# Another front for a fused conditioning block: the first weight block in halves, the second summed on TensorE, the turn later, and a grouped last bias

## The reference, cut to what matters

```
h = ln(ln(x, pw_g[path], pw_b[path]), cp_g[class], cp_b[class])
t = ln(x, tm_g[class], tm_b[class]);  s = ln(x, ms_g[scale], ms_b[scale])
m, n, r = x + (one row per batch, from three small networks)
cat = [w0*h, w1*t, w2*m, w3*n, w4*r, w5*s]
out = x + ln(silu(cat @ int_W1 + int_b1) @ int_W2 + int_b2, int_g, int_be)
```

## Time and profile before

| what | us |
|---|---|
| runs, median of 3 (lowest, highest) | 931.65 (930.84, 932.00) |
| the profiled execution, its own time | 931.71 |
| its span, first to last instruction | 930.0 |
| PE busy | 920.1 (99%) |
| DVE busy | 825.4 (89%) |
| POOL busy | 478.7 (51%) |
| ACT busy | 327.0 (35%) |

### The profile page before, as it was taken

One profiled execution on the slowest core, in us unless ns is written; L12 is line 12 of the kernel. 1 busy time (PEld: TensorE's weight loads), 2 busy tenths in 40 slices (PEclk: granted clock), 3 DMA queues, 4 the chain that ended last, 5 costly groups with the idle time before them and its releaser, 6 DMA issues.

```text
span 930.0 us, 13476 instructions
## 1 busy us (share of the span) xinstructions
PE 920.1 (99%) x4178; PEld 746.5 (80%) x4178; DVE 825.4 (89%) x1205; ACT 327.0 (35%) x414; POOL 478.7 (51%) x577
## 2 busy tenths in 40 slices
PE   8999999999999999999999999999999999999997
PEld 7777888888888888888888888887888878788885
DVE  7889999798989989899898989989899898989965
ACT  5835234252332514324242333424224242333412
POOL 5456474544736455474644637454473644637240
PEclk9999999999999999999999999999999999999999
DMA  9984666738666574756748566574757648565541
GB/s 334 349 307 153 215 171 244 187 95 262 165 217 176 162 236 132 252 133 239 189 118 262 162 213 160 184 226 121 251 144 243 175 128 254 160 218 155 136 113 45
DMA packets 99619, 178.75 MB, mean 192 GB/s; under 512 B 10129, under 2 KB 49041, under 8 KB 95633
## 3 DMA queue, kind: packets, MB, share of 16 engines
q1 hardware_dynamic: 44512, 95.88, 29.9%
q0 software_dynamic: 22976, 66.07, 27.1%
q10 hardware_dynamic: 32112, 16.58, 6.1%
HBM read 145.75 MB, written 32.75 MB: 192 GB/s over the span
## 4 chain that ended last, share of the span: by engine, by line
DVE 32%; PE 29%; DMA 16%; issue 12%; POOL 4%; ACT 3%; ACTq 2%; DVEq 1%; POOLq 0%; SPq 0%
DMA h_turned<-y_sb 15%; PE hid_ps L1612 7%; PE hid_ps L1614 7%; PE hid_ps L1613 7%; DVE y_sb L1117 4%; DVE yst L1120 4%; DVE r_sb L1216 4%; ACT v_ring L800 3%; DVE xc L1028 3%; DVE hid_lo L1141 3%; DVE v_ring L1080 3%; POOL fve L544 2%; DVE fst L1152 2%; DVE cat_lo L1010 2%; DVE o_sb L1150 2%
## 5 line engine op out<-in xcount | busy, mean ns | idle before, releaser
L1612 PE MATMUL hid_ps<-cat_hi,w_hi 128*128 128x512 f32 x1008 | 395.0, 392 | 0.0
L1614 PE MATMUL hid_ps<-cat_hi,w_lo 128*128 128x512 f32 x1008 | 392.3, 389 | 0.0
L1613 PE MATMUL hid_ps<-cat_lo,w_hi 128*128 128x512 f32 x1008 | 392.3, 389 | 0.0
L1612 PEld LDWEIGHTS hid_ps<-cat_hi,w_hi 128*128 128x128 f32 x1008 | 189.2, 188 | 47.4 <-issue 7.4
L1614 PEld LDWEIGHTS hid_ps<-cat_hi,w_lo 128*128 128x128 f32 x1008 | 189.2, 188 | 39.5
L1613 PEld LDWEIGHTS hid_ps<-cat_lo,w_hi 128*128 128x128 f32 x1008 | 189.3, 188 | 38.6
L617 POOL DMA_INDIRECT pw_rows<-pw,path_now x64 | 73.1, 1142 | 123.4 <-DVE y_sb L1136 106.7
L638 POOL DMA_DIRECT2D r_sb<-x x60 | 57.5, 958 | 135.1 <-DVE r_sb L1216 129.7
L624 POOL DMA_INDIRECT pw_rows<-cp,class_now x64 | 94.7, 1480 | 35.3 <-issue 12.6
L846 ACT ACTIVATE cat_hi<-v_ring 128x1024 fp32r<-128x1024 f32 x30 | 31.9, 1063 | 193.4 <-DMA v_ring<-h_turned 191.8
L838 ACT ACTIVATE cat_hi<-v_ring 128x1024 fp32r<-128x1024 f32 x64 | 66.5, 1060 | 84.6 <-DVE v_ring L1080 37.9
(11 more groups left out here) (197 smaller groups left out, 1378.3 us busy)
## 6 DMA issues: line engine op xcount, KB each, us to landing
x_sb<-xp SPq DMA_DIRECT2D x16, 1024.0 KB
out<-r_sb SPq DMA_DIRECT2D x63, 256.0 KB, 2.0
xc<-xT SPq DMA_DIRECT2D x15, 1024.0 KB
h_turned<-y_sb ACTq DMA_DIRECT2D x60, 256.0 KB
r_sb<-x POOLq DMA_DIRECT2D x60, 256.0 KB, 4.5
v_ring<-h_turned SPq DMA_DIRECT2D x60, 256.0 KB, 2.9
stats_bc<-token_stats SPq DMA_DIRECT2D x15, 512.0 KB, 5.8
ids_sb<-ids SPq DMA_DIRECT2D x16, 256.0 KB
```

The costliest lines, as they stand in the source:

```text
L1612: pe.matmul(acc, w1_hi[:, k, cols], hi, start=start, stop=False)
L1613: pe.matmul(acc, w1_hi[:, k, cols], lo, start=False, stop=False)
L1614: return pe.matmul(acc, w1_lo[:, k, cols], hi, start=False, stop=stop)
```

## The change

It replaces the front. The two loads of weight block 0 become two column halves of all three source blocks (384 KB each); x^T's first half comes as two loads of one feature block. Block 0 is summed, rounded and multiplied in column halves. Block 1 is summed by PE: three f32 matmuls with w2, w3, w4 on a diagonal (`mix_diag`, made by POOL) into `made_ps`; its high and low parts are read from there. Block 2 now stands ahead of `turn_x(0)` on PE, block 3 ahead of `turn_x(1)`; ACT rounds block 2 before it norms x, and block 3 before it copies the turned half. 23 warm matmuls stand first, none later. The last bias becomes four matmuls of 32 rows each, on four row groups, together ahead of `last_second(0)`; POOL prepares it for all 128 rows. In the loop, `out_sum(b-1, 0)` and `out_stats(b-1, 1)` move ahead of `y_mul(b+1, 0)` and `y_mul(b+1, 1)`.

SP, POOL and the constants (the last part is POOL's preparation of the last bias):

```diff
-WARM = (30, 7)
+WARM = 23
+
+HALF = D // 2
...
+        mix_diag = [stats_bc[:, j, 0:P] for j in range(NETS)]
...
-                    sp.dma_start(keep[:, 0, :], blocks[:, 0, :]).then_inc(sum_in[k], 16)
-                    sp.dma_start(keep[:, 1:NETS, :], blocks[:, 1:NETS, :]).then_inc(sum_more_in[k], 16)
+                    for i in range(2):
+                        cols = slice(i * HALF, (i + 1) * HALF)
+                        sp.dma_start(keep[:, 0:NETS, cols], blocks[:, :, cols]).then_inc(part_in[i], 16)
...
+                pool.wait_ge(mix_ready, 1)
+                for j in range(NETS):
+                    pool.tensor_tensor(mix_diag[j], ident, w_mix[:, 2 + j:3 + j].to_broadcast([P, P]), ALU.mult).then_inc(diag_ready, 1)
                 pool.wait_ge(signs_ready, 2)
...
-            pool.memset(class_tab[:, :].bitcast(f32), 0.0).then_inc(b2_cleared, 1)
-            pool.memset(onehot[:, 0:P].bitcast(f32), 1.0).then_inc(b2_cleared, 1)
...
-                pool.tensor_copy(class_tab[at:at + 1, :], b2_bc[at:at + 1, :]).then_inc(b2_rounded, 1)
...
+            pool.memset(onehot[:, 0:P].bitcast(f32), 1.0 / 8).then_inc(b2_cleared, 1)
...
+            pool.tensor_copy(class_tab[:, :], b2_bc).then_inc(b2_rounded, 1)
...
+            pool.tensor_tensor(b2_low, in_cols[0], in_cols[1].bitcast(f32), ALU.subtract).then_inc(b2_rounded, 1)
...
+            pool.tensor_tensor(b2_high, in_cols[1].bitcast(f32), high_rows, ALU.mult).then_inc(b2_rounded, 1)
...
+            pool.tensor_tensor(b2_low, b2_low, low_rows, ALU.mult).then_inc(b2_rounded, 1)
...
+            pool.tensor_tensor(in_cols[1], b2_high, b2_low, ALU.add).then_inc(b2_ready, 1)
```

ACT's order:

```diff
-            sum_first(0)
-            x_high(0, 0)
-            sum_high(0)
-            sum_first(1)
+            part_first(0)
+            x_first_high(0)
+            part_first(1)
+            part_high(0)
+            x_first_high(1)
+            part_high(1)
             x_high(0, 1)
+            sum_high(1)
+            sum_first(2)
             act.wait_ge(table_in, 16)
             act.activation(class_tab[:, :], tab_raw, ACT.Copy).then_inc(tab_rounded, 1)
+            sum_high(2)
             act.wait_ge(tab_rounded, 1)
             act.activation(class_tab[:, :], class_tab[:, :].bitcast(f32), ACT.Copy, scale=tab_sign).then_inc(tab_hi_done, 1)
-            sum_high(1)
-            sum_first(2)
             for t in range(TT - 1):
                 x_norm(t)
-            sum_high(2)
             sum_first(3)
+            sum_high(3)
             xhat_copy(0)
-            sum_high(3)
```

DVE's order in `first_chunk` and in `chunk`:

```diff
-                sum_blocks(0)
-                x_low(0, 0)
-                sum_low(0)
+                part_sum(0)
+                x_first_low(0)
+                part_low(0)
+                part_sum(1)
+                part_low(1)
+                x_first_low(1)
                 gain_signs()
                 for t in range(TT):
                     x_stats(0, t)
-                sum_blocks(1)
                 x_low(0, 1)
                 sum_low(1)
+                sum_blocks(2)
                 x_norm_last()
-                sum_blocks(2)
+                sum_low(2)
                 tab_low()
                 onehot_first()
-                sum_low(2)
                 sum_blocks(3)
...
+                out_sum(b - 1, 0)
+                out_stats(b - 1, 1)
                 if not (first or last):
                     y_mul(b + 1, 0)
-                out_sum(b - 1, 0)
-                if not (first or last):
                     y_mul(b + 1, 1)
-                out_stats(b - 1, 1)
```

PE's new functions and its order:

```diff
+            def block_sum():
+
+                pe.wait_ge(diag_ready, NETS)
+                pe.wait_ge(sum_in[1], 16)
+                for j in range(NETS):
+                    ins = pe.matmul(made_ps[:, 1, :], mix_diag[j], keep[:, NETS + j, :], start=(j == 0), stop=(j == NETS - 1))
+                ins.then_inc(block_summed, 1)
...
+            def last_bias():
+
+                pe.wait_ge(o_done, TT * (BATCHES - 1))
+                pe.wait_ge(b2_ready, 1)
+                for t in range(TT):
+                    rows_of = slice(GROUP * t, GROUP * (t + 1))
+                    pe.matmul(second_ps[t], onehot[rows_of, 0:P], class_tab[rows_of, :], start=True, stop=False)
...
-                warm(WARM[0])
-                x_high_part(0)
-                x_low_part(0)
-                warm(WARM[1])
+                warm(WARM)
+                first_products(0)
+                first_products(1)
+                block_sum()
                 x_high_part(1)
                 x_low_part(1)
+                x_high_part(2)
+                x_low_part(2)
                 turn_x(0)
-                x_high_part(2)
                 first_fill(0)
-                x_low_part(2)
-                turn_x(1)
                 x_high_part(3)
                 x_low_part(3)
+                turn_x(1)
                 nets_hidden()
```

More of the change, by code:

```diff
@@ L437, in spread_stats @@
                 wait(sp, xhat_done, b - 1)
+                if isinstance(b, int) and b == 1:
+                    sp.wait_ge(block_summed, 1)
                 part_of = stats_dram.rearrange("(g m) i -> g (m i)", m=32)[:, 0:2 * P]
@@ L830, in x_high @@
             def x_high(b, i):
[L831 removed]
+                act.wait_ge(xT_in, 16 * (b + 1))
                 wait(act, used, 6 * (b - 1) + 5 + i)
@@ L1011, in x_low, with x_first_low, part_sum, part_low @@
                                   cat_hi[:, slot(i), :, :].bitcast(f32), ALU.subtract).then_inc(x_lo_done, 1)
+            def x_first_low(k):
+                dve.wait_ge((first_x_hi, x_hi_done)[k], 1)
+                dve.tensor_tensor(cat_lo[:, 0, k, :], xc[:, k, :], cat_hi[:, 0, k, :].bitcast(f32),
+                                  ALU.subtract).then_inc((first_x_lo, x_lo_done)[k], 1)
+            def part_sum(i):
+                cols = slice(i * HALF, (i + 1) * HALF)
+                dve.wait_ge(part_in[i], 16)
+                dve.wait_ge(sum_begun, i + 1)
+                for j in (1, 2):
+                    dve.scalar_tensor_tensor(w1_raw[:, 0, cols], keep[:, j, cols], w_mix[:, 2 + j:3 + j], w1_raw[:, 0, cols],
+                                             ALU.mult, ALU.add).then_inc(sum_done, 1)
+                    dve.wait_ge(sum_done, 2 * i + j)
+            def part_low(i):
+                cols = slice(i * HALF, (i + 1) * HALF)
+                dve.wait_ge(sum_hi_done, i + 1)
+                dve.tensor_tensor(w1_lo[:, 0, cols], w1_raw[:, 0, cols], w1_hi[:, 0, cols].bitcast(f32),
+                                  ALU.subtract).then_inc(sum_lo_done, 1)
             def turn_stats(b):
@@ L1649, in warm, with first_products @@
                     pe.matmul(o_ps[:, 1, 0:P], sel_all, sel_all, start=True, stop=True)
+            def block_sum():
[4 more added lines that the diff above has]
+                ins.then_inc(block_summed, 1)
+            def first_products(i):
+                hi, lo = cat_hi[:, 0, 0, :], cat_lo[:, 0, 0, :]
+                two = range(2 * i, 2 * i + 2)
+                if i == 0:
+                    pe.wait_ge(first_x_hi, 1)
+                pe.wait_ge(sum_hi_done, i + 1)
+                for h in two:
+                    pe.matmul(hid_ps[:, h, :], w1_hi[:, 0, h * P:(h + 1) * P], hi, start=True, stop=False)
+                if i == 0:
+                    pe.wait_ge(first_x_lo, 1)
+                for h in two:
+                    pe.matmul(hid_ps[:, h, :], w1_hi[:, 0, h * P:(h + 1) * P], lo, start=False, stop=False)
+                pe.wait_ge(sum_lo_done, i + 1)
+                for h in two:
+                    pe.matmul(hid_ps[:, h, :], w1_lo[:, 0, h * P:(h + 1) * P], hi, start=False, stop=False)
             def x_high_part(k):
                 hi, lo = cat_hi[:, slot(k // 2), k % 2, :], cat_lo[:, slot(k // 2), k % 2, :]
-                pe.wait_ge(sum_hi_done, k + 1)
+                pe.wait_ge(sum_hi_done, k + 2)
                 pe.wait_ge(x_hi_done, k // 2 + 1)
                 for h in range(FT):
-                    pe.matmul(hid_ps[:, h, :], w1_hi[:, k, h * P:(h + 1) * P], hi, start=(k == 0), stop=False)
+                    pe.matmul(hid_ps[:, h, :], w1_hi[:, k, h * P:(h + 1) * P], hi, start=False, stop=False)
                 pe.wait_ge(x_lo_done, k // 2 + 1)
```

64 lines of the change are left out of this document (42 added, 22 removed).

## The result

The changed kernel takes **932.98 us** (median of 13 runs, 932.61 to 933.35); before takes 931.19 beside it (13 runs, 930.33 to 932.4). The ratio is **1.0018** with an interval of 1.0011 to 1.0025: slower by 1.8 us. The profiled execution takes 933.02, with a span of 931.3 against 930.0.

A forecast was written before the change was run, and what follows sets the result against it. PE was taken to bound 30.8 to 912 us, leaving front and tail. Front +1.3, loop 0, tail -0.35 give +0.95 on the profiled 931.71: 932.66, forecast 932.6 as median; range 930.8 to 935.2, likeliest case 932.0 to 934.2.

The forecast's parts named there:

- The chain from T to nets_hidden: Front, through block 3, the turn and its copy: ACT, DVE and PE steps in series take T + 12.2 us.
- T: Front: the end of DVE's `sum_blocks(2)`, forecast at 18.45 us, with ends at 18.1 and 18.9.
- half B: Front: second column half of weight block 0, forecast to land at about 7.7 us and be summed by 9.85.
- The front's term: Front up to `nets_hidden`: start at 30.65 instead of 29.36, a cost of +1.3 us (+0.9 to +1.8, or +2.2).
- The loop: The 13 passes: moved DVE work falls into the wait for h and gains no time; 0 (0 to +0.3 us).
- Block 1 on PE: Front: PE's f32 sum starts with the load at 12.1, takes 2.65 us; block 1 runs from 15.4 to 18.2.
- The tail: Last bias to the end: four grouped biases take 0.53 instead of 0.91; end moves by -0.35 us (0 to -0.57).
- A: Rival, chance 0.3: clock falls in PE's new front gaps, a dip costing up to 1.7 us; 934.3, or 935.0 with two.
- B: Rival, chance 0.14: front's ACT and DVE chain is shorter, PE's work decides; `nets_hidden` 1.35 us before 29.36, time 930.0.
- C: Rival, chance 0.06: split loads make half B land 1.3 us later in the front; T moves by 1.0, time 933.6.
- Half B's latency: Front: splitting weight block 0's loads adds no latency to half B, counted as nothing; full fixed DMA cost would give 934.3.

The follow-up runs named there:

- e7: Changed kernel with `turn_x(1)` ahead of block 3 on PE and `xhat_copy(0)` ahead of `sum_high(3)` on ACT: 929.99 us, ratio 0.9979 to before.
- e5: Changed kernel with x^T's first half in one load of 4 KB runs again: 931.98 us, ratio 0.9999 to before.
- e6: Changed kernel with ACT's `part_high(1)` ahead of `x_first_high(1)`, x^T still in two loads: 932.32 us, ratio 1.0004 to before.
- e1: Kernel before with only DVE's new loop order: 929.17 us, ratio 0.999 to before.
- e12: Kernel before with only DVE's new loop order, run again on another chip: 929.23 us, ratio 0.9994 to before.
- e9: Kernel before, old front, with DVE's new loop order and the grouped last bias: 928.86 us, ratio 0.9989 to before.
- e8: Changed kernel with x^T's half in one load, `part_high(1)` ahead of `x_first_high(1)` and `turn_x(1)` ahead of block 3: 929.32 us, ratio 0.9973 to before.
- e10: Kernel before with new loop order, grouped bias and 15 instead of 7 warm matmuls between blocks 0 and 1: 928.88 us, ratio 0.999 to before.
- e11: Changed kernel with x^T's first half in one load and `turn_x(1)` ahead of block 3, ACT's order kept: 929.13 us, ratio 0.9991 to before.

## Why the prediction was right, and where it was not

**The chain from T to nets_hidden: right.** Worked out 12.2, measured 12.31, with each idle time of PE within 0.3 us. That the turn behind block 3 is bare was shown by e7, which took 2.94 us off by moving it.

**T: the term that was mis-sized.** The prediction had half B decide DVE's front and took it that x^T comes as before. Half B was in time (ACT's row at 8.27 has no wait); the load that had no term in the sum, x^T's second feature block, came at 11.34. The step said of DVE "free for `x_stats` at 11.35"; it was 13.46. With T = 20.21 in place of 18.45 its own rule gives 32.41 for `nets_hidden`, 0.11 from the measurement. e5 and e6 split the cause: of 1.76 us, 1.16 go with the load made whole, 0.79 with ACT's order alone. Both undo the same wait, by its cause or by its consequence, and in e6 the load of block 2, 0.9 later than worked out, is the next limit. With x^T whole T is still 19.05, 0.6 above 18.45, and no run takes this rest apart. Three things are later by the rows of e5: the small constants (4.85 against 4.40), x^T's first block (7.66 against 7.39), and DVE's `class_columns`, here in the changed kernel with POOL beside it, and before:

```profile
6.31 0.99 DVE L1330 CAST class_cols<-small_sb 128x80 fp32r<-128x80 f32 x4
...
6.48 1.12 POOL L598 TENSOR_TENSOR stats_bc<-small_sb 128x128 f32<-128x128 f32 x3
```

```profile
5.78 0.54 DVE L1270 CAST class_cols<-small_sb 128x80 fp32r<-128x80 f32 x4
```

The casts take nearly twice as long beside POOL's diagonals. The prediction asked only when the diagonals are done and put them at no cost. The front's term was +1.3 with an upper end of +2.2; it measured +3.16.

**The loop: the step that failed.** The prediction said of the ground that DVE gains that "none reaches the time, because PE did not wait for DVE". PE did, in four chunks of the profiled execution, by up to 0.6 us each. The busy time of the stretch, 881.09 of 881.20, could not show it, since ends of matmuls are modelled and rows overlap. The prediction saw DVE's 2.48 us wait for h and that the moved work falls into it, and stopped there. It did not ask whether DVE's own round is shorter than PE's. e1 shows the gain to be the order's. In the four traces with the old order the first five to ten chunks are even, and then most are long, but not all: the size of the gain varies with the execution.

**Block 1 on PE: the price right, the place not.** Six instructions in 2.73 us, 2.65 taken. They start at 13.82, behind half B's late products, and not at 12.1 with the load, so block 1 runs from 17.24 instead of 15.4. POOL's three diagonals end at 7.6, long before 13.82.

**The tail: nearly right.** -0.35 said, -0.20 from the picks and -0.29 from the bias measured; the four biases take 0.43 up to the next matmul, where 0.33 and 0.1 on that side were counted. DVE's last statistics lie 3.01 apart, as said. POOL's five operations end at 909.35, before PE needs them at 913.58, though they take 6.15 us in all.

**Rivals.** A: no fall of the clock in the changed kernel, in spite of seven idle times of 0.4 to 1.3 us. It was the old front that paid, in a share of its executions. The price was mis-sized too, at 1.7 us: `nets_hidden` starts at 29.36 and 29.38 with the dip (before, e12) and at 28.24 and 28.40 without it (e1, e9), so 1.0 to 1.1. B: the chain was as long as counted. C: its mechanism, a split load that lands late, happened to a load other than the one it named, with T later by more than its 1.0; its price at the end was paid off by the loop.

**Half B's latency: rightly counted at nothing.** ACT takes it at 8.27 without a wait, behind x^T's first block. The Trainium skill (DMA: Bandwidth & Descriptors, Anatomy of one DMA) gives a fixed cost of about 2.0 us for a DMA that GpSimd starts; half B is started by SP. Charged in full to half B that would make 934.3, as an estimate from the page's figure, and ACT's row at 8.27 speaks against such a charge here.

**A comparison over chips.** The ratios of e7 and e8 (0.9979, 0.9973) look better than e9's (0.9989), but their before was at 932.23, and e9's at 930.04. What varies is before: its long chunks and its dip occur in some executions and not in others. Its lowest run in the third group, 928.88, is as fast as e12's lowest, 928.92. Kernels with the loop order and no idle time of 2.4 us in the front vary by 0.3 to 1.0 us from lowest to highest (after, e5 to e8, e10, e11), before by 2.1 to 4.9 in its four groups of runs. So e9's and e10's 928.9 is the lowest median of all, 0.1% under before; against the changed kernel it is about 0.3% lower, worked out from the two ratios and not measured side by side.

## What to carry to other kernels

For each engine that works in rounds, compare the length of its round with that of the bound engine, by the distance of the same row in two chunks far apart: a round that is 0.3 us too long on average costs nothing while the slack lasts, five to ten chunks here, and then in most chunks, and busy time will not show it. Fill a wait for a transfer with work that is independent of it. When a load is split, look at every load of that stretch and at what stands behind its consumer in the in-order queue; and work that PE pays bare at the end of a chain (a turn and its copy) belongs ahead of matmuls that can cover it.

## What the runs showed of the hardware

- The same idle time of 2.36 us on PE was followed by half clock in some executions (five of eleven runs of e12 by their times and mean clocks, three of e9) and not in others. With it cut to 0.52 (e10) or broken up (e11), none of 22 runs showed a mean clock of 0.997. One profile doesn't tell how often a dip comes: here it is 1.0 to 1.1 us times its share.
- 512 KB of x^T landed at 7.7 as one load and at 11.3 as two, beside the same loads of SP. One such landing differs by 0.6 us between two executions (7.66 in e5, 8.25 in e8).
- Four casts of 128x80 on DVE took 0.99 us beside POOL's 128x128 products and 0.54 without them. From the first cast to the last product of `class_columns` it is 1.54 us in all seven traces with the diagonals and 0.96 to 0.98 in the seven without.
- A short stop of PE costs more than itself: after each of the two waits above, the first matmul is followed by the next after 0.34 us instead of 0.23, so a wait of 0.07 us costs 0.18. In the records of 512-column matmuls 0.23 apart a wait below 0.16 us leaves no idle time at all.
